# Probabilities turned in 32x32 blocks by VectorE and regrouped by SBUF-to-SBUF DMAs, instead of turned by TensorE, in an attention and ternary-FFN kernel

## What is computed

```
xn  = layernorm(x)
xh  = layernorm(xn) * ln_w + ln_b
q, k, v = xh @ W_q[h] + b_q, xh @ W_k[h] + b_k, xh @ W_v[h] + b_v       # 16 heads of 64
p   = softmax(where(causal, q @ k.T / 8, -inf))                        # 256 x 256 for each head
att = sum over h of (p @ v) @ W_o[h]  + b_o
ffn = relu(xn @ Wq1.T + b1) @ Wq2.T + b2      # Wq1, Wq2: W1, W2 rounded to -1, 0, 1 by their mean size
out = x + att + ffn
```

## Time and profile before

| | |
|---|---|
| median of 3 runs | 269.41 us (269.0 to 269.49) |
| the profiled execution's own time | 270.71 us |
| its span | 268.7 us |
| granted TensorE clock | 1.00 throughout (2.4 GHz) |
| busy: TensorE, VectorE, ScalarE, GpSimd | 97%, 87%, 83%, 79% of the span |
| DMA | 5.72 MB in all, nearly all in the first 20 us |

### The profile page before, as it was taken

The page is one execution under the profiler, slowest core; times in us unless marked ns, Lnnn a source line. Parts: engine busy times, 40 slices in busy tenths (PEclk is TensorE's granted clock), DMA queues, the critical chain, the costliest instruction groups (busy, mean ns, idle before and its releaser), DMA issues.

```text
span 268.7 us, 7430 instructions
## 1 busy us (share of the span) xinstructions
PE 259.7 (97%) x2420; PEld 226.8 (84%) x2420; DVE 233.4 (87%) x1006; ACT 222.8 (83%) x798; POOL 212.0 (79%) x431
## 2 busy tenths in 40 slices
PE   6989899999999999999999999999999999999994
PEld 5767688799888998899897998889887998989874
DVE  2799999998999899997999899998999979997841
ACT  3589997988888997988978988889969889996950
POOL 5489999999859979599768979599786997576750
PEclk9999999999999999999999999999999999999999
DMA  7980000000000000000000000000000000000000
GB/s 166 257 206 1 1 2 4 0 1 2 22 1 2 0 23 1 4 0 2 20 4 4 0 2 20 4 2 2 20 2 1 2 1 22 0 4 0 22 2 20
DMA packets 12737, 5.72 MB, mean 21 GB/s; under 512 B 6790, under 2 KB 12444, under 8 KB 12700
## 3 DMA queue, kind: packets, MB, share of 16 engines
q1 hardware_dynamic: 12656, 5.25, 8.1%
...
## 4 chain that ended last, share of the span: by engine, by line
PE 87%; DVE 4%; POOL 3%; ACT 2%; DMA 1%; issue 0%; SPq 0%; POOLq 0%; ACTq 0%
PE m_ps L846 11%; PE s_ps L812 11%; PE m_ps L825 6%; PE m_ps L787 6%; PE m_ps L850 5%; PE m_ps L832 5%; PE m_ps L826 5%; PE m_ps L788 5%; PE m_ps L789 5%; PE s_ps L817 5%; PE m_ps L873 3%; PE m_ps L799 3%; PE m_ps L800 2%; PE m_ps L801 2%; DMA wq_raw<-in_L_attn_W_q 1%; PE m_ps L877 1%
## 5 line engine op out<-in xcount | busy, mean ns | idle before, releaser
L604 DVE CUSTOM_DVE_ANT_0 s_ps<-s_ps,causal 128x256 f32<-128x256 f32 (+1 forms) x256 | 84.8, 379 | 0.0
L465 ACT ACTIVATE prob<-s_ps,neg_max 128x256 f32<-128x256 f32 x128 | 65.4, 511 | 8.4 <-DVE neg_max L604 8.4
L384 POOL TENSOR_SCALAR prob<-prob,inv_sum 128x128 f32<-128x128 f32 x128 | 48.4, 378 | 24.1 <-DVE inv_sum L611 24.1
L386 POOL TENSOR_SCALAR prob<-prob,inv_sum 128x256 f32<-128x256 f32 x128 | 61.8, 483 | 0.0
L467 ACT ACTIVATE prob<-s_ps,neg_max 128x128 f32<-128x128 f32 x128 | 52.3, 409 | 0.0
L473 ACT ACTIVATE pT_wide<-m_ps 128x512 f32<-128x512 f32 x64 | 38.6, 606 | 16.2 <-PE m_ps L826 16.0
L377 POOL TENSOR_TENSOR qk_first<-k_all 128x128 f32<-128x128 f32 x64 | 29.1, 461 | 14.8 <-DVE k_all L592 14.7
L812 PE MATMUL s_ps<-k_all,q_last 64*128 64x256 f32 x384 | 39.2, 310 | 0.3 <-ACT prob L467 0.3
L846 PE MATMUL m_ps<-pT_wide,v 128*64 128x256 f32 x256 | 39.3, 385 | 0.0
L604 DVE DVE_READ_ACCUMULATOR2_ANT neg_max<- 128x1 f32 x256 | 36.2, 141 | 0.0
L812 PEld LDWEIGHTS s_ps<-k_all,q_last 64*128 64x128 f32 x384 | 26.9, 185 | 9.3 <-issue 7.7
...
## 6 DMA issues: line engine op xcount, KB each, us to landing
out<-out_sb SPq DMA_DIRECT2D x8, 128.0 KB, 1.8
...
bv_all<-in_L_attn_b_v SPq DMA_DIRECT2D x1, 512.0 KB, 6.1
...
wo<-in_L_attn_W_o SPq DMA_DIRECT2D x1, 512.0 KB, 6.1
```

The lines of the kernel that those rows point to most:

```text
L384: nc.gpsimd.tensor_scalar(prob[:, j, h, S:W], prob[:, j, h, S:W], inv_sum[:, j, 2 + h:3 + h], 0.0, ALU.mult, ALU.add)
L386: last = nc.gpsimd.tensor_scalar(prob[:, j, h, 0:S], prob[:, j, h, 0:S], inv_sum[:, j, h:h + 1], 0.0, ALU.mult, ALU.add)
L465: nc.scalar.activation(prob[:, j, h, 0:S], s_ps[:, pair % 2, h, 0:S], ACT.Exp, bias=neg_max[:, j, h:h + 1], scale=-1.0, accum_out=row_sum[ ...
L604: last = nc.vector.tensor_tensor_reduce(out=sc, in0=sc, in1=mask, scale=-SCALE, scalar=-MASKED, op0=ALU.add, op1=ALU.min, accum_out=neg_ma ...
```

## The change

- **Scores.** `q` and `k` of a pair are written whole in fp32 by ACT alone (tile `qk`); DVE's `pr` (L589, L592) and POOL's `k` (L377) are gone. All scores are one whole fp32 matmul for each head and query tile. The keys are read in the order `g j k`, which takes every fourth token, 16 bytes apart: the key on column 32j+k of a tile is token 4k+j. The causal mask is built in that order.
- **Turning.** `tw`, `tn` and their copies are gone. DVE turns a pair's 768 columns in 32x32 blocks from `prob` to `blocks` (step `t`). For each duo the SP queue issues four DMAs (step `d`), one for each block of 32 queries: each reads 32 partitions of 6144 bytes and writes 1536 bytes to each of 128 partitions of `pT`, 196,608 bytes, so 786,432 bytes for a duo. `z` waits for them. A pair's `t` waits for its division `p`; `d` of a duo waits for its second `t` and for `z` of the same duo one batch earlier.
- **Host.** Weights, FFN weights and vectors arrive in the layout in which they are used (rows of 1 KB and more), x arrives a second time turned, and the output is stored turned: TensorE's turns of the output, the vectors and the FFN weights and ACT's copies of them are gone, and DVE adds bias and turned x in one instruction.
- **Order.** All lists are new, and SP has one.

```diff
--- before.py
+++ after.py
...
+BUSY = (12, 5)
+PE_HEAD = ("xa:0 xb:1 pr0:0 pr1:3 pr2:1 pr3:2 s0 s1 v0:2 pr4:0 s2 ta:3 s3 xn:2 v1:3 pr5:0 pr6:1 pr7:2 f0:2 s4 s5 "
+           "s6 v2:2 v3:3 f1:1 xh+:2 s7 z0:2 pr0+:0 pr1+:3 pr2+:1 pr3+:2 s0+ s1+ z1:1 v0+:2 pr4+:0 s2+ s3+ xn+:2 "
+           "v1+:3 pr5+:0")
+PE_PLAN = ("pr6:1 pr7:2 oa-:0 f0:2 s4 s5 z2-:3 z3-:1 s6 v2:2 v3:3 f1:1 xh+:2 ob- s7 z0:2 pr0+:0 pr1+:3 pr2+:1 "
+           "pr3+:2 s0+ s1+ z1:1 v0+:2 pr4+:0 s2+ s3+ xn+:2 v1+:3 pr5+:0")
+PE_TAIL = ("pr6:1 s4 z2-:2 pr7:1 s5 z3-:0 s6 oa-:1 s7 ob- f0:2 v2:0 z0:3 f1:1 z1:2 v3:1 z2:1 oa:2 z3:1 ob")
+ACT_HEAD = ("wh0 wh1 wh2 xa wh3 wh4 pr0 pr1 pr2 pr3 e0 e1 e2 aa wh5 oh e3 pr4 e4 xn pr5 pr6 e5 pr7 e6 e7 e8 e9 f0 "
+            "e10 e11 e12 xh+ f1 e13 e14 z0 e15 pr0+ pr1+ pr2+ pr3+ e0+ e1+ e2+ e3+")
+ACT_PLAN = ("z1- pr4 e4 xn pr5 pr6 e5 pr7 e6 e7 e8 e9 z2- f0 z3- e10 e11 e12 xh+ f1 e13 e14 z0 e15 pr0+ pr1+ pr2+ "
+            "pr3+ e0+ e1+ e2+ e3+")
+ACT_TAIL = ("z1- pr4 e4 xn e5 pr5 pr6 e6 e7 e8 z2- e9 pr7 e10 e11 z3- e12 e13 e14 f0 e15 f1 z0 z1 z2 z3")
+DVE_HEAD = ("lz nh wl0 wl1 wl2 xb wl3 xl m0 m1 m2 m3 v0 i0 m4 th te0 te1 i1 xn m5 m6 ln+ t0 m7 v1 t1 i2 m8 m9 m10 "
+            "m11 i3 t2 i4 v2 m12 m13 i5 t3 xh+ m14 v3 i6 m15 z0 t4 t5 t6 m0+ m1+ m2+ i7 m3+ v0+ i0+ m4+ t7")
+DVE_PLAN = ("z1- i1 xn m5 m6 ln+ t0 m7 v1 t1 i2 m8 m9 m10 m11 z2- i3 t2 z3- i4 v2 m12 m13 i5 t3 xh+ m14 o- v3 i6 "
+            "m15 z0 t4 t5 t6 m0+ m1+ m2+ i7 m3+ v0+ i0+ m4+ t7")
+DVE_TAIL = ("m5 i1 z1- m6 i2 t0 xn m7 m8 t1 m9 t2 i3 z2- m10 i4 m11 t3 m12 i5 m13 z3- t4 m14 t5 o- i6 m15 v1 i7 "
+            "t6 t7 v2 z0 v3 z1 z2 z3 o")
+POOL_HEAD = ("bo hs np vl0 g0 g1 p0 vl1 ol")
+POOL_PLAN = ("p1- ln p2- p3- p4- h0- xl p5- p6- p7- h1- p0")
+POOL_TAIL = ("p1- ln p2- p3- h0- p4- xl p5- p6- p7- h1- p0 p1 p2 p3 p4 p5 p6 p7 h0 h1")
+SP_HEAD = ("d0 d1 d2 d3 d0+ d1+ st d2+ d3+")
+SP_PLAN = ("d0+ d1+ st d2+ d3+")
+SP_TAIL = ("st")
...
+        qk = sb("qk", [P, NBUF, 2, S])
...
-        o_part = sb("o_part", [D, S])
-        out_sb = sb("out_sb", [P, TILES, D])
+        xT_cur = sb("xT_cur", [D, 2, S])
+        out_sb = sb("out_sb", [D, 2, S])
 
         W = S + P
-        prob = sb("prob", [P, NBUF, 2, W])
-        pT_wide = sb("pT_wide", [P, NBUF, 2, S])
-        pT_narrow = sb("pT_narrow", [P, NBUF, 2, P])
+        prob = sb("prob", [P, NBUF, 2, QT, 3, QB])
+        blocks = sb("blocks", [P, DUOS, QT * 3, 2, 2, QB])
+        pT = sb("pT", [P, DUOS, QT, 3, 2, 2, QB])
...
+            def load_weights(n):
+                name, cols = PARTS[n]
+                sp.dma_start(raw[name][:, cols], {"q": w_q, "k": w_k, "v": w_v}[name][:, cols]).then_inc(w_in[n], 16)
...
+            def regroup(b, duo):
+                wait(sp, turned, PAIRS * b + 2 * duo + 2)
+                wait(sp, z_psd, DUOS * (b - 1) + duo + 1)
+                for i in range(QT):
+                    rows = slice(i * QB, i * QB + QB)
+                    sp.dma_start(pT[:, duo, i, :, :, :, :].rearrange("p g n h q -> p (g n h q)"),
+                                 blocks[rows, duo, :, :, :, :].rearrange("k c n h q -> k (c n h q)")
+                                 .rearrange("k (j r) -> k j r", j=QT)).then_inc(pT_in[duo], 16)
+            def store(b):
+                wait(sp, o_done, b + 1)
+                sp.dma_start(outT[b], out_sb[:, b % 2, :]).then_inc(out_done[b % 2], 16)
+                if b + 2 < B:
+                    load_turned(b + 2)
...
+            diagonal = causal[:, P:S].rearrange("p (j k) -> p j k", j=QT)
+            nc.gpsimd.affine_select(out=diagonal, in_=diagonal, compare_op=ALU.is_ge, fill=MASKED,
+                                    base=0, pattern=[[-1, QT], [-QT, QB]], channel_multiplier=1).then_inc(consts, 1)
...
+                for n, col in enumerate((BQ + pair, BK + pair)):
+                    last = nc.scalar.activation(qk[:, j, n, :], halves("pr", pair, b)[:, n, :], ACT.Identity,
                                                 bias=vecs[:, col:col + 1])
-                last.then_inc(qk_hi, 1)
...
+                nc.scalar.activation(prob[:, j, h, :, 1:3, :].rearrange("p j g k -> p g j k"),
+                                     s_ps[:, pair % 2, h, 0:S].rearrange("p (g j k) -> p g j k", g=2, j=QT), ACT.Exp,
+                                     bias=neg_max[:, j, h:h + 1], scale=-1.0, accum_out=row_sum[:, j, h:h + 1])
+                nc.scalar.activation(prob[:, j, h, :, 0, :], s_ps[:, pair % 2, h, S:W].rearrange("p (j k) -> p j k", j=QT),
+                                     ACT.Exp, bias=neg_max[:, j, 2 + h:3 + h], scale=-1.0,
                                      accum_out=row_sum[:, j, 2 + h:3 + h]).then_inc(exp_done, 1)
...
+            def turn_blocks(b, pair):
+                wait(dve, prob_ready, PAIRS * b + pair + 1)
+                duo, n = divmod(pair, 2)
+                wait(dve, pT_in[duo], 16 * QT * b)
+                nc.vector.transpose(blocks[:, duo, :, n, :, :], prob[:, pair % NBUF, :, :, :, :]
+                                    .rearrange("p h j g k -> p (j g) h k")).then_inc(turned, 1)
...
+                nc.vector.scalar_tensor_tensor(out=out_sb[:, b % 2, :], in0=bank("oa", 0, b)[:, 0:S],
+                                               scalar=out_bias[:, :], in1=xT_cur[:, b % 2, :], op0=ALU.add, op1=ALU.add)\
+                    .then_inc(o_done, 1)
...
+                k_blocks = qk[:, pair % NBUF, 1, :].rearrange("e (g k j) -> e g j k", g=TILES, j=QT)
+                wait(pe, qk_ready, PAIRS * b + pair + 1)
                 wait(pe, exp_done, 2 * PAIRS * b + 2 * (pair - 2) + 2)
                 j = pair % NBUF
-                for q_at, k_at in ((LO, HI), (HI, LO), (HI, HI)):
+                for queries, tiles, at in ((slice(P, S), slice(0, 2), slice(0, S)), (slice(0, P), slice(0, 1), slice(S, W))):
                     for h in range(2):
                         rows = slice(h * E, h * E + E)
-                        nc.tensor.matmul(s_ps[:, pair % 2, h, 0:S], q_last[rows, j, q_at, :], k_all[rows, j, k_at, :],
-                                         start=(q_at == LO), stop=((q_at, k_at) == (HI, HI)))
-                wait(pe, k_whole, PAIRS * b + pair + 1)
-                for h in range(2):
-                    rows = slice(h * E, h * E + E)
-                    last = nc.tensor.matmul(s_ps[:, pair % 2, h, S:W], qk_first[rows, j, 0, :], qk_first[rows, j, 1, :],
-                                            start=True, stop=True)
+                        last = nc.tensor.matmul(s_ps[:, pair % 2, h, at], qk[rows, j, 0, queries], k_blocks[rows, tiles, :, :],
+                                                start=True, stop=True)
                 last.then_inc(s_psd, 1)
...
+                pe.wait_ge(pT_in[duo], 16 * QT * (b + 1))
                 dst = halves("z", duo, b)
                 for n in range(2):
                     pair = 2 * duo + n
                     for h in range(2):
                         cols = slice((2 * pair + h) * E, (2 * pair + h) * E + E)
-                        nc.tensor.matmul(dst[h * E:h * E + E, n, :], v[:, 0, cols], pT_wide[:, pair % NBUF, h, :],
-                                         start=True, stop=False)
+                        nc.tensor.matmul(dst[h * E:h * E + E, n, :], v[:, 0, cols],
+                                         pT[:, duo, :, 0:2, n, h, :].rearrange("p i g q -> p g i q"), start=True, stop=False)
                     for h in range(2):
                         cols = slice((2 * pair + h) * E, (2 * pair + h) * E + E)
-                        last = nc.tensor.matmul(dst[h * E:h * E + E, n, P:S], v[:, 1, cols],
-                                                pT_narrow[:, pair % NBUF, h, :], start=False, stop=True)
+                        last = nc.tensor.matmul(dst[h * E:h * E + E, n, P:S], v[:, 1, cols], pT[:, duo, :, 2, n, h, :],
+                                                start=False, stop=True)
...
+    return {"x": x, "xT": x.transpose(0, 2, 1), "w_q": by_input(w_q), "w_k": by_input(w_k), "w_v": by_input(w_v),
+            "w_o": w_o.reshape(PAIRS, P, D).transpose(1, 0, 2).reshape(P, PAIRS * D), "w1T": w1.T,
+            "w2T": w2.T.reshape(FC, P, D).transpose(1, 0, 2).reshape(P, FC * D), "columns": columns,
+            "b_v": b_v.reshape(1, H * E)}
```

More of the change, by code:

```diff
@@ L45 @@
[L45 to L63, removed]
@@ L300, in _ @@
-            sp.dma_start(wo[:, :, :], w_o.rearrange("(p two) e d -> (two e) p d", two=2)).then_inc(wo_in, 16)
-            sp.dma_start(x_all[:, 2 * TILES:NT, :], x_v[:, 2 * TILES:NT, :]).then_inc(x_in[2], 16)
-            out_v = out.rearrange("b (t p) d -> b p t d", p=P)
-            for b in range(B):
-                sp.wait_ge(ot_done, b + 1)
-                sp.dma_start(out_v[b], out_sb[:, :, :]).then_inc(out_done, 16)
-            sp.wait_ge(out_done, 16 * B)
+            load_weights(5)
@@ L309, in _ @@
+            def store(b):
[3 more added lines that the diff above has]
+                    load_turned(b + 2)
```

(22 more changed lines are left out.)

285 lines of the change are left out of this document (77 added, 208 removed).

## The result

| | before | after |
|---|---|---|
| median of the runs | 269.45 us (4 runs) | 290.2 us (4 runs, 288.11 to 291.79) |
| ratio, with its 95% interval | | 1.0764 [1.069, 1.0838] |
| profiled execution, its span | 270.71, 268.7 us | 289.66, 287.9 us |

One execution in this document, one of run 8's four at 248.2 us, fell in a slower state of the chip; the median of its other three is 245.36 us.

What follows compares the result with a forecast made beforehand. TensorE's own work was taken to bound the kernel. Start 40.5, six periods of 26.3 and end 30.6 gave a 228.9 us span; with 0.7 over it, a median of 229.6 us, range 222 to 251.

Steps and rivals of the forecast that it cites:

- Rival 1: Scores' keys read 16 bytes apart halve TensorE's pace: 5.2 us more a batch, about 270 us in all; chance 8%.
- The start: Stretch before TensorE's repeated list: first maximum at 11.6 us, then VectorE's summed work, list beginning at 40.5 us.
- 8.0 us for the first projection: At the start, first projection moves from 9.07 to 8.0 us, as turned vectors and weights in 256-byte pieces go.
- The ternary step: In VectorE's work at the start, ternary weights and norms were counted at 3.3 us.
- The period: One batch of the repeated list: 26.3 us, bounds 25.8 to 27.5, including 0.2 us for waits.
- TensorE's 26.1: TensorE's work per batch: 31.0 us, less 5.4 for turns, plus 0.5 for whole-fp32 scores.
- VectorE's turn: Block turn of a pair's 768 columns on VectorE: 0.9 us, bounds 0.6 and 1.7, eight a batch.
- rival 2: VectorE's block turn goes at half pace, 1.7 us, making VectorE the bound at 31.2 us a batch: 267; chance 7%.
- Rival 3: VectorE and GpSimd shut each other out during block turns: period 28.9 us, 250 us in all; chance 9%.
- The DMAs: Regrouping of turned blocks: 4.6 us for a duo, bounds 1.8 and 9.2, hidden in the repeated list.
- the shortest cover of the layout: Least time in a batch between a duo's second block turn and its z: 6.9 us, for duo 1.
- The end: Tail after the repeated list, from VectorE's last maximum to the final store's landing: 30.6 us.

Runs made afterwards that it cites:

- run 8: On top of run 3, ScalarE forms high parts of the second-half value weights and the output weights after the fifth exponential; 246.13 us, ratio 0.9157.
- run 6: On top of run 3, ScalarE reads PSUM at a step of 4 elements and writes keys to neighbouring SBUF places; 244.23 us, ratio 0.9061.
- run 11: Kernel before the change, with the three fp32r passes of its wide scores reading keys at a step of 4 elements; 287.83 us, ratio 1.0671.
- step 2: Kernel before the change, first tile's whole-fp32 scores reading keys at a step of 2 elements (8 bytes); 270.08 us, ratio 1.0017.
- step 4: Kernel before the change, first tile's whole-fp32 scores reading keys at a step of 4 elements (16 bytes); 282.49 us, ratio 1.0459.
- run 9: On top of run 3, the edits of run 6 and run 8 together; 243.94 us, ratio 0.9048.
- run 1: Changed kernel, but ScalarE writes a pair's keys in the order in which the scores read them; 256.93 us, ratio 0.952.
- run 2: Changed kernel, but batch 0's first pair no longer waits for low parts of the weights' second half; 280.97 us, ratio 1.0404.
- run 7: On top of run 3, the 128 DMAs regrouping turned blocks are left out and TensorE reads the blocks directly; 246.61 us, ratio 0.9146.
- run 3: Changed kernel with the edits of run 1 and run 2 together; 247.56 us, ratio 0.9163.

## Why the prediction was wrong, point by point

**The rival was in the prediction, and its dismissal was the error.** Rival 1 had 8%. Against it I had set that a whole fp32 product takes 0.43 us for the columns that an fp32r pass streams in 0.117, "so it asks for a column less often than TensorE can read one". This is the step that failed. The rows say x4 for two products, and narrower windows of the same timeline show how the four lie: two records, one for each head, start together, and the next two 0.21 us later (0.216 on the median).

```profile
132.92 0.38 PE L846 MATMUL m_ps<-pT_wide,v 128*64 128x256 f32 x2
```
```profile
133.13 0.39 PE L846 MATMUL m_ps<-pT_wide,v 128*64 128x256 f32 x2
```

So a product is two records of 0.216 us each, and the slack was at most that of 0.216 against 0.117, and not of 0.43; the row could not exclude the rival. The runs show that there was no slack at all. The wide scores of the kernel after, 256 columns, whose next record stands at 105.87:

```profile
104.90 0.70 PE L753 MATMUL s_ps<-qk 64*128 64x256 f32 x2
```
```profile
105.42 0.63 PE L753 MATMUL s_ps<-qk 64*128 64x256 f32 x2
```

The first record, behind other work, takes 0.52 us and the second 0.45; with neighbouring keys (run 6) these are 0.32 and 0.22. An fp32r record of 256 columns went from 0.118 to 0.233 (run 11). If a whole fp32 record read its columns once, slowly, a reading of 0.233 us would have lengthened its 0.216 by very little; instead it doubled, as the fp32r record did. That it reads its columns twice at full pace would explain this; the trace doesn't show the two readings apart. The Trainium skill (Advanced Engine Details and Errata, SBUF Cachelines) wants at least two hits on a 16-byte line: the runs agree (step 2 all but free, ratio 1.0017; step 4 dear, 1.0459). That rule spoke for the rival, and the row, read rightly, gave nothing firm against it.

**Its price** was put at 5.2 us a batch, and that was right: the scores take 11.75 us of TensorE in a batch and 6.5 to 6.8 in run 9. The periods differ by 4.6 (31.77 against 27.2 in run 1) to 5.0 us (26.8 in run 9). Of the whole it is 33.3 us in run 1, which pays for the scattered write, and some 36.6 with that put right (run 6), a little below the 38 to 40. Rival 1's 270 was missed by 20 because the start was wrong besides.

**The start** was predicted at 40.5 and was 63.1. The first failed step is 8.0 us for the first projection: I took its inputs to be what it waited for, and hadn't read what the changed condition in `project` leaves to pair 0. It cost 9.2 us (run 2), the fallen clock behind the 6.88 us of standing still included. The ternary step was counted at its unhindered length, though the earlier trace rows show VectorE held by GpSimd; it was held for 1.0 and 2.0 us, which in run 8 gave nothing that can be told. What is left is 48.4 against 40.5 in run 9. The prediction laid out VectorE alone, as if it never waited, and it was busy only 33 of 40 us there; and it put the clock at nothing, where run 9 spends some 7 us at the lower level. Which of the waits among the four engines is worth how much, and how much of it the clock makes, stays open.

**The period.** With neighbouring keys 26.8 to 26.9 us is measured against 26.3. TensorE's 26.1 was nearly right because two errors met: in run 9's batch from 130.52 to 157.23 us the scores take 6.5 us and not 5.2, and all the rest 20.2 and not 20.9. A pair takes 0.76 to 0.88 us instead of 0.65: its first record takes 0.32 us and not 0.22 when other work stands ahead, and its last narrow one 0.21 and not 0.11. The row I took, `z`, has weights of 64 columns, the scores of 128. I haven't shown that this is the reason.

**VectorE's turn** was put at 0.9 us, from the copy of 512 columns. It takes 955 ns, so rival 2 is out. The other estimate beside it, 0.98 us, is close too, but the prediction doesn't give the fixed part that it must have used:

```profile
L576 DVE STREAM_TRANSPOSE blocks<-prob 128x768 f32<-128x768 f32 x64 | 60.0, 955 | 0.8 <-POOL prob L386 0.8
```

**Rival 3**, that VectorE and GpSimd shut each other out during turns, didn't happen: the turns keep 955 ns on average, and GpSimd's division instructions 379 and 487 ns, where the kernel before has 378 and 483.

**The DMAs** were hidden, as said: run 7 shows it. But the 4.6 us for a duo was too low: from the issue of its first DMA to the landing of its last it takes 6.1 us in the kernel after (median), since SP issues one only every 0.66 us. That lies inside the shortest cover of the layout, 6.9 us, but not by much: in the shorter batches of runs 6 and 9 TensorE waits for them for 2.2 and 0.8 us in all between 75 and 208 us. The row of a single DMA, median from issue to landing, lies inside the 3 to 5 us given:

```profile
pT<-blocks SPq DMA_DIRECT2D x128, 192.0 KB, 3.7
```

**The end** was 34.1 us against 30.6. Most of this goes with the strided keys: with neighbours it is 31.4 us in run 3 and 31.7 in run 9, and the four pairs of scores in the tail cost 1.53 us each instead of some 0.86, 2.7 us together. The remaining 1 us isn't taken apart.

**The sum of it:** 290.2 - 229.6 = 60.6 us. Strided keys 33.3, the first pair's wait 9.2, the scattered write that stands in for them 3.3 (run 6 against run 3; 2.8 by the ratios), and about 14 left in run 9. Of its profiled span, 241.7 against 228.9, 7.9 stand at the start, 3.7 in the six periods and 1.1 at the end.
